# Deeper row fetch for the routed expert blocks of a GNN and mixture-of-experts kernel

## What is computed

```python
# layer 1, on layernorm(x)
rh = relu(features @ router_w1 + router_b1)
expert_logits = softmax(rh @ router_w2 + router_b2)
top_w, top_i = top_k(expert_logits, 2); routing_weights = softmax(top_w)
h1 = relu(einsum('bsd,edh->bseh', features, expert_w1) + expert_b1)   # 6 experts, 256 -> 256
h2 = relu(einsum('bseh,ehf->bsef', h1, expert_w2) + expert_b2)        # 256 -> 256
expert_out = einsum('bsef,efo->bseo', h2, expert_w3) + expert_b3      # 256 -> 256
x = x + sum(take(expert_out, top_i) * routing_weights)
# layer 2, on layernorm(layernorm(x)) with gamma and beta: 8 experts, top 2
h = gelu(xn @ W1[e] + b1[e]);  y_e = h @ W2[e] + b2[e]                # 256 -> 512 -> 256
x = x + sum over the two chosen e of y_e * w[e]
```

## Time and profile before

| | us |
|---|---|
| median of 3 runs | 3053.35 (3052.78 to 3055.44) |
| profiled execution, its own time | 3075.53 |
| its span, first to last instruction | 3073.9 |
| PE busy | 2233.9 (73%) |
| DVE busy | 1752.6 (57%) |
| ACT busy | 1109.5 (36%) |
| POOL busy | 569.4 (19%) |
| mean granted TensorE clock | 0.838 |

### The profile page before, as it was taken

The page is one execution under the profiler, slowest core; times in us unless marked ns, Lnnn a source line. Parts: engine busy times, 40 slices in busy tenths (PEclk is TensorE's granted clock), DMA queues, the critical chain, the costliest instruction groups (busy, mean ns, idle before and its releaser), DMA issues. The chain is left out here.

```text
span 3073.9 us, 43892 instructions
## 1 busy us (share of the span) xinstructions
PE 2233.9 (73%) x12743; PEld 1686.6 (55%) x12744; DVE 1752.6 (57%) x4284; ACT 1109.5 (36%) x2048; POOL 569.4 (19%) x897
## 2 busy tenths in 40 slices
PE   5877886694683924774779359975588888569998
PEld 1233444353571513664349258863477777458887
DVE  7998885315346064445224745534777787545554
ACT  0244774101431002553124125631323323147765
POOL 2332331000302021563100126640100000000000
PEclk6798887796896966887899669986799999679999
DMA  1112343310001202443310125531212221000001
GB/s 42 52 69 119 154 171 130 118 69 5 23 4 70 104 4 90 138 135 112 137 62 1 40 90 156 157 100 49 89 55 70 83 67 50 11 12 21 21 21 34
DMA packets 134696, 225.35 MB, mean 73 GB/s; under 512 B 18141, under 2 KB 101342, under 8 KB 134420
## 3 DMA queue, kind: packets, MB, share of 16 engines
q1 hardware_dynamic: 121159, 187.11, 17.9%
q0 software_dynamic: 13392, 36.33, 4.1%
HBM read 146.00 MB, written 77.39 MB: 73 GB/s over the span
## 5 line engine op out<-in xcount | busy, mean ns | idle before, releaser
L2193 DVE SCALAR_TENSOR_TENSOR att_masked<-dinv_row,att_thr,x_feat 128x512 fp32r<-128x512 f32 x400 | 278.0, 747 | 109.8 <-PE att_ps L2305 94.7
L318 PE MATMUL count_ps<-hot_key,hot_lo 128*128 128x320 f16 x960 | 282.9, 356 | 50.0 <-DVE hot_key L300 28.9
L2305 PE MATMUL att_ps<-att_xl_parts,att_masked 128*128 128x260 f32 x1600 | 267.9, 314 | 58.4 <-DVE att_masked L2193 55.6
L1914 DVE TENSOR_TENSOR e_h_low<-x_feat,e_h_high 128x512 fp32r<-128x512 f32 (+1 forms) x240 | 169.5, 709 | 244.9 <-ACT e_h_high L1839 244.9
L299 DVE TENSOR_SCALAR hot_lo<-o_tok,key_stage 128x128 f16<-128x128 f16 x960 | 260.4, 271 | 48.2 <-POOL key_stage L281 45.0
L300 DVE TENSOR_SCALAR hot_key<-o_tok,key_stage 128x320 f16<-128x320 f16 x960 | 284.9, 297 | 0.2 <-issue 0.2
L797 PE MATMUL g_ps<-g_at,g_y 128*128 128x512 f16 x1170 | 261.7, 386 | 29.5 <-DMA g_at<-counts_t_high 23.9
L2305 PEld LDWEIGHTS att_ps<-att_xl_parts,att_masked 128*128 128x128 f32 x1600 | 223.9, 202 | 101.3 <-DVE att_masked L2193 75.4
L1838 ACT ACTIVATE x_feat<-e_hps,e_b 128x512 f32<-128x512 f32 (+1 forms) x240 | 177.6, 740 | 202.0 <-issue 99.5
L318 PEld LDWEIGHTS count_ps<-hot_key,hot_lo 128*128 128x128 f16 x960 | 97.6, 102 | 223.6 <-DVE hot_key L300 205.8
L797 PEld LDWEIGHTS g_ps<-g_at,g_y 128*128 128x128 f16 x1170 | 115.6, 99 | 173.2 <-DMA g_at<-counts_t_high 24.9
(11 more groups left out here) (469 smaller groups left out, 5103.5 us busy)
## 6 DMA issues: line engine op xcount, KB each, us to landing
g_at<-counts_t_high SPq DMA_DIRECT2D x12, 2560.0 KB
x_feat<-counts_high SPq DMA_DIRECT2D x40, 640.0 KB, 4.1
e_w_in<-in_L_ffn_W SPq DMA_DIRECT2D x34, 512.0 KB
counts_t_high<-turn_high SPq DMA_DIRECT2D x20, 640.0 KB, 3.0
counts_t_low<-turn_low SPq DMA_DIRECT2D x20, 640.0 KB, 4.2
counts_high<-row_high SPq DMA_DIRECT2D x20, 640.0 KB, 3.0
counts_low<-row_low SPq DMA_DIRECT2D x20, 640.0 KB, 4.1
e_w_in<-in_L_ffn_expert_w SPq DMA_DIRECT2D x45, 256.0 KB
```

Source lines behind the costliest of these rows:

```text
L318: pe.matmul(acc[:, q % 4, 0:KW], hot_lo[:, j, :], hot_key[:, j, :], start=False, stop=False, skip_group_check=True).then_inc(slot_free, 1)
L1914: dve.tensor_tensor(h_parts[i][1][:, v % 2, f, 0:w], h_sb[i][:, f, 0:w], h_parts[i][0][:, v % 2, f, 0:w].bitcast(F32), ALU.subtract).then_ ...
L2193: dve.scalar_tensor_tensor(S[:, n % RING, :], EL[:, it % 2, u - 1, :], thr[:, t, h:h + 1], A[:, t, :], ALU.is_gt, ALU.mult).then_inc(maske ...
L2305: mm = pe.matmul(ps[:, n % 2 * TB + q, 0:PW], side[:, q * P:(q + 1) * P], moving, start=(t == 0), stop=(t == NT - 1))
```

## The change

The ring of fetched rows gets four buffers instead of two. POOL fetches `NH + 4` blocks ahead of the put instead of `NH + 2`, and `fetch(b)` waits for the turning of block b - 4. The output bias gets a semaphore of its own, so that TensorE waits for the hidden bias rows alone ahead of its bias transposes; SyncE waits for the output bias at the end of its list.

```diff
@@ phase_routed
-    counted, ranked, hot_high, hot_part, hot_low, ordered, rows_in, bias_turned, known = (
+    counted, ranked, hot_high, hot_part, hot_low, ordered, rows_in, bias_turned, known, bo_in = (
...
                         sp.dma_start(r.bo_sb[:, :, :].rearrange("p e d -> p (e d)"),
-                                     bout.rearrange("e d -> (e d)").partition_broadcast(P)).then_inc(rows_in, 16)
+                                     bout.rearrange("e d -> (e d)").partition_broadcast(P)).then_inc(bo_in, 16)
...
-                        sp.wait_ge(rows_in, 16 * (NH + 1))
+                        sp.wait_ge(bo_in, 16)
...
-                        pe.wait_ge(rows_in, 16 * (NH + 1))
+                        pe.wait_ge(rows_in, 16 * NH)
@@ routed_blocks
-    XB = YB = 2
+    XB, YB = 4, 2
...
-                ahead = NH + 2
+                ahead = NH + XB
```

More of the change, by code:

```diff
@@ L1132, in phase_routed @@
         sem(f"{name}_{s}") for s in ("loaded", "dve", "want_exp", "exped", "logits", "pe_hid", "act_hid", "consts"))
-    counted, ranked, hot_high, hot_part, hot_low, ordered, rows_in, bias_turned, known = (
+    counted, ranked, hot_high, hot_part, hot_low, ordered, rows_in, bias_turned, known, bo_in = (
         sem(f"{name}_{s}") for s in ("counted", "ranked", "hot_high", "hot_part", "hot_low", "ordered", "rows_in",
-                                     "bias_turned", "known"))
+                                     "bias_turned", "known", "bo_in"))
     held_in = [sem(f"{name}_held_in{i}") for i in range(2)]
```

## The result

| | before | after |
|---|---|---|
| median of the runs, us | 3053.07 (3046.68 to 3055.44, 4 runs) | 3016.17 (3013.52 to 3019.70, 4 runs) |
| ratio | | 0.9883 [0.9865, 0.9901] |
| profiled execution, us | 3075.53 | 3016.79 |
| its span, us | 3073.9 | 3015.1 |
| mean granted clock | 0.838 | 0.842 |

The change saves 37 us. The forecast was 64, and 3016.2 lies above the range too. Against the *profiled execution* of before, though, 58.8 us of span are gone. (The profiled execution of after is one of its four runs; that of before, 3075.53, is none of its four.)

The account below looks back on a forecast made before the run. TensorE's waits for rows fetched late on POOL's list, and the slow clock behind them, were taken as the bound. Savings of 42 us (layer 1) and 22 us (layer 2), 64 in all, gave 2989.4 us; 8-in-10 range 2980 to 3012.

Parts of the forecast that it names:

- What bounds the kernel, and why the rows are late: Block loops: TensorE waits 34.7 and 14.6 us for rows whose fetch stands behind a put on POOL's list; buffers aren't missing.
- Fetch distance: Both layers' block loops: fetched rows are used two stages later, 13.4 us to spare; all TensorE waits for rows should go.
- Layer 2: Fourteen stages of layer 2 at 12.2 us each, 170.8 instead of 193.2 us: 22 us saved.
- Layer 1: Eleven stages of layer 1 at 9.6 us each, 105.6 instead of 147.7 us: 42 us saved.
- POOL as the next bound: Layer 1: at 1.333 us an issue POOL falls behind 1.06 us a stage, within the spare; PE still sets the end.
- Rival 1: POOL paces layer 1, its issues lengthened under DVE subtractions: 34 and 20 us saved in the layers, 2999 us; chance 0.19.
- Rival 3: Block loops: each DVE subtraction of two SBUF tiles stops POOL for its whole length; about 9 us slower, 3062; chance 0.03.
- More fetches ahead of put 0: Layer 1's start: eight more issues, 10.7 us, covered by POOL's 11.88 us of idleness; DVE not held by puts, no cost.
- The bias semaphore: Bias transposes: output bias had already landed, so no gain and no loss; 0, within 1 us either way.
- The sum's transfer: Both block loops: the 64 us read from the profiled execution come off the 3053.35 us median too, giving 2989.4 us.

Follow-up runs that it names:

- buffers_alone: Kernel before with four buffers of fetched rows but the fetch at its old place on POOL's list; 3054.45 us, 1.0011 of before.
- place_alone: Kernel before with its two row buffers kept, but the fetch one block further ahead on POOL's list (NH + 3); 3018.30 us, 0.9890 of before.
- before_again: Kernel before, unchanged, run and profiled once more; 3049.59 us, 0.9997 of before, profiled execution 3049.28 us.
- psum_h: Changed kernel with each activation's second copy written into its PSUM tile instead of SBUF, so h's subtraction has one SBUF input; 3006.36 us, 0.9853 of before.
- puts4: Changed kernel with four result buffers for the puts instead of two; 3013.20 us, 0.9882 of before.
- bias_alone: Kernel before with only the semaphore for the output bias, old rings and fetch distance kept; 3049.81 us, 0.9999 of before.

## Why the prediction was wrong, by its own steps

*What bounds the kernel, and why the rows are late:* right. buffers_alone leaves 29.8 us of waits in layer 1, place_alone 11.2, and none in layer 2.

*Fetch distance:* the waits went in layer 2 altogether and in layer 1 up to block 10.

*Layer 2:* right in the stage, 12.2 us forecast and 12.09 measured. The saving fits only the profiled execution: 23.9 of its 193.2 us (22 forecast, bound 23.6), but 10.8 of before_again's 180.1.

*Layer 1:* 42 us were forecast against the profiled execution, 35.4 came. The stages themselves are faster than the 9.6 us I took: 9.23, near the clean stage of the earlier trace rows, and ACT was no bound (busy for 56.86 / 7 = 8.1 us a stage). Its idleness for "remote", which I had put on each stage, isn't there. But the last four stages take 47.7 us, 10.8 more than four of 9.23. The 112.3 us so hold two errors of opposite sign: 4.1 less than I took for stages, 10.8 more for waits and the clock behind them.

*POOL as the next bound:* two terms are mis-sized. The price of an issue, 1.333 us, measured 1.505, since DVE's subtractions of two SBUF tiles stretch the issues that start inside them, and both engines got denser. The landing, taken at 2.0 us, measured 4.1, 4.2 and 3.9 for blocks 11, 13 and 14, and the trace of before already had 4.0. At 1.333 the 64 issues from 1252.58 to the fetch of block 14 would end at 1337.9, and its rows be ready 2.0 us (my figure) to 4.1 later, at 1339.9 to 1342.0. TensorE would want them at 1303.58 + 4 x 9.23 = 1340.5. So with stages of 9.23 us instead of 9.6 the spare was used up at my price already, and 0.17 us an issue made POOL the bound. psum_h shows it: at 1.325 every wait is gone. (Its put 0 stands 10.8 us behind the turn of block 3, 13.6 in after, but that isn't what did it: from 1253.98, 64 issues of 1.505 us end at 1350.3, behind the 1344.9 at which block 14 is turned there.) Where the added landing comes from, no run asked. Rival 1 happened, in four of eleven stages. Rival 3, the same mechanism in full, would have needed 1.84 us an issue.

The rule of the Trainium skill that stood beside that rival (page "SBUF — State Buffer", section "Who interferes with whom") names the right pair of engines. The runs agree with it that two SBUF inputs are what matters (psum_h). They agree on the blocking too where the subtraction came first: all 28 stretched issues end 0.82 to 0.92 us behind the one that they start inside. They don't where the issue came first: the subtraction at 1302.30 begins 0.30 us into an issue that lasts to 1302.99. And not every subtraction meets a starting issue: POOL lost 17 us to some 49 us of them, and the mean issue grew by 0.17 us and not by the 0.5 of rival 3.

*More fetches ahead of put 0:* put 0 does start late, at 1252.58 behind the fetches, without a wait for DVE, and DVE waits 28.7 us for its buffers, which I had excluded. (The spare there is 1254.6 less 1241.5, 13.1 us less 1.1 b; the 14 was a slip without effect.) By puts4 this costs nothing that can be told.

*The bias semaphore:* nothing, as forecast (bias_alone).

*The sum's transfer is the step that failed:* "the loops are made of the same stages in each, so the same 64 come off 3053.35". The loops of the profiled execution were not those of the median run. before_again has 139.9 and 180.1 us for the stages that took 147.7 and 193.2: 20.9 us of what I meant to save isn't in it, and 7.8 + 13.1 of them lie in layers 1 and 2. The account closes, by one profiled execution of each: 64 less 20.9, less 6.7 (112.3 instead of 105.6 in layer 1), plus 1.5 (169.3 instead of 170.8 in layer 2) gives 38; 37 were measured. So the transfer is the larger error, 20.9 us, and POOL's terms, 10.8 us less the 4.1 of the stages, the smaller. Against the profiled execution the same sum missed by only 5 us, 3011.5 forecast and 3016.8 measured. That is in part luck: 3016.8 was measured without the idleness for "remote" that the base had, and where after has such idleness too, it took 3055.1.

The sign of it was in the rows. The profiled execution stood 22 us above the median, 0.7%, and the earlier trace rows hold "remote" idleness in the very stretch in question. I noted both, used the one as a cost of ACT and carried the other over as if it lay elsewhere. With the 22 us taken to lie in the two loops, and to be absent from the runs of after, the forecast would have been 3011.5, 5 us from the result.

## What to carry to other kernels

Before a saving read from one profiled execution is carried to the median, ask where their difference lies and whether it is one of those runs at all; if the difference may lie in the stretches that the change touches, the saving shrinks by it. When data is late, look at what stands ahead of its issue on the queue before adding buffers: one place earlier gave here what two more buffers couldn't. An issue price read while an engine had gaps was too low here once it had none (1.333 against 1.505 us), beside subtractions with both inputs in SBUF; and a time to landing read once, at 2.0 us, was half of the 4.1 that counted.

## What the runs showed of the hardware

An indirect issue on POOL takes 0.95 to 1.0 us alone, and in after up to 2.02 in layer 1 and 3.02 in layer 2 where it starts inside a DVE subtraction of two SBUF tiles (the earlier trace rows are such a pair); each such stretched issue ends 0.81 to 0.92 us behind the subtraction. Issues of that trace that had started before the subtraction weren't stretched (1302.00). With one of the inputs in PSUM the mean of layer 2's fetches fell from 1.434 to 0.961 us.

The same kernel took 3050, 3073 or 3084 us on different chips. The profiled executions on the latter two show idleness of ACT, DVE and POOL inside the block loops with no releaser in the trace, 62 to 110 us in all, and on the one at 3073 half of the change's gain was gone. Its cause is open.
